# Attention loop written out, and probabilities times values as float32 products of 32 columns

## The chip, the core and the metric

The kernel runs on one core of a Trainium2 chip. The core has five engines that run side by side and wait for each other by semaphores: TensorE (PE in the profile; its weight loads are PEld), VectorE (DVE), ScalarE (ACT), GpSimd (POOL) and SyncE (SP), which here only issues transfers. Products are written to PSUM, the accumulation memory; everything else is read from SBUF. The metric is device time in microseconds, the median of three executions.

## The reference

A gated block in two parts, for 16 sequences of 256 tokens and width 512: cross attention with 16 heads of 32 columns and a causal mask, then a mixture of 8 experts, of which each token takes 6, and a shared expert. Only the attention is touched:

```python
q = x @ Wq.T;  k = context @ Wk.T;  v = context @ Wv.T
scores = jnp.einsum('bhqd,bhkd->bhqk', q, k) * SCALE
scores = jnp.where(causal[None, None, :, :], scores, -jnp.inf)
probs = jax.nn.softmax(scores, axis=-1)
y = jnp.einsum('bhqk,bhkd->bhqd', probs, v)
y = y.transpose(0, 2, 1, 3).reshape(b, t, c)
return y @ Wo.T + bo
```

with `x` replaced by its layer norm ahead of it and added to `tanh(g)` times the result behind it.

## The kernel before

`attention` works through the 16 sequences, called batches here. Each engine has its own program, in which `run(i)` stands for one turn and walks through 16 slots, `s` = 0 to 15, one for each head. In turn `i` the scores of batch `i` are made; between them, spread over the slots, stand the projections of batch `i + 1` (K in slots 0 to 3, Q in 4 to 7, V in 8 to 11) and the output projection of batch `i - 1` (slots 12 to 15). Turns run from -1 to 16. The order on each engine is thus written by hand; nothing is planned by costs. `iterations` (from line 226) writes turns -1 to 2 out, runs 3 to 12 in a loop of five passes of two turns over a register, and writes 13 to 16 out.

TensorE in slot `s` (`run`, from line 718): the scores of head `s`, two matmuls of 256 columns (L727), which contain three passes over stacked high and low parts; the products of probabilities and values of head `s - 4` (L744 to L746); three 128x128 transposes of the probabilities of head `s - 2` (L753); then the slot's part of a projection (L626 in `three_pass`, L616 for transposes). Full products are built from rounded parts: a value is split into a high and a low part, and hi x hi, hi x lo and lo x hi are summed.

Between the transposes and the products stand two engines. ScalarE copies the transposed probabilities to `pt_hi` in float16 (L452), VectorE subtracts it from PSUM for `pt_lo` (L591). Values are held in three bfloat16 parts in `v_parts`: ScalarE makes the first (L418), VectorE the remainder `v_rest` (L567), ScalarE the second from it (L422), GpSimd the third (L368). A head has three pairs of a query block and a key block below the diagonal, and each pair takes three 16-bit products: pt_hi with the first two parts (64 columns), pt_hi with the third (32), pt_lo with the first two (64). They fill two column groups in PSUM, which VectorE adds in `close_group` once for four heads (L531), before it multiplies by the inverse row sums (L535).

VectorE besides makes the mask, the maximum and the scaling of the scores (L559); ScalarE the exponentials (L457, L459). The experts' part (`experts`) holds the only float32 product of the kernel: `transpose_back` (L1174), in which four matmuls per block turn the logits back with the 16 rows of `fold`.

Of the kernel before, what the change touches and what calls it, by code (L numbers as in the profile page):

```python
# [21 lines left out]
F16 = mybir.dt.float16  # L22
# [6 lines left out]
P = 128  # L29
# [101 lines left out]
def attention(nc, ctx, memory, x, ctx_t, g_xattn, g_ffn, wq_t, wk_t, wv_t, wo_t, bo, x1, x1_stored, ident, gates, tanh_gates):  # L131
# [34 lines left out]
    v_parts = [sb(f"v_parts{i}", [P, T, 3, D], BF16) for i in range(2)]  # L166
    v_rest = sb("v_rest", [P, D])
    RING = 4
    probs = [sb(f"probs{i}", [P, 3 * P]) for i in range(RING)]
    pt_hi = [sb(f"pt_hi{i}", [P, 3 * P], F16) for i in range(2)]  # L170
    pt_lo = [sb(f"pt_lo{i}", [P, 3 * P], F16) for i in range(2)]
# [4 lines left out]
    y_sum = sb("y_sum", [P, T * JH, DH])  # L176
# [13 lines left out]
    y_ps = [psum(f"y{i}", [P, T, JH, 2, DH]) for i in range(2)]  # L190
# [8 lines left out]
    pool_chain, rstd_made, c_lo_made, v3_made = sem("pool_chain"), sem("rstd_made"), sem("c_lo_made"), sem("v3_made")  # L199
# [7 lines left out]
    v1_made, v2_made, yt_hi_made = sem("v1_made"), sem("v2_made"), sem("yt_hi_made")  # L207
    probs_made, pt_hi_made = sem("probs_made"), sem("pt_hi_made")
# [4 lines left out]
    v_rest_made, yt_lo_made, x1_made = sem("v_rest_made"), sem("yt_lo_made"), sem("x1_made")  # L213
    max_made, pt_lo_made, y_made = sem("max_made"), sem("pt_lo_made"), sem("y_made")
# [12 lines left out]
    FIRST, PAIRS = 3, 5  # L227

    def iterations(eng, run):

        for i in range(-1, FIRST):
            run(At(0, 2, i))
        with eng.Fori(0, PAIRS) as r:
            for u in range(2):
                run(At(r, 2, FIRST + u))
        for i in range(FIRST + 2 * PAIRS, B + 1):
            run(At(0, 2, i))
# [23 lines left out]
    V_SLOTS, V_EVAC, V_SPLIT = ((8, 9), (10, 11)), (10, 12), (11, 13)  # L263
# [17 lines left out]
    def build(start):  # L281
        with nc.Block() as block:
# [57 lines left out]
            def _(pool):  # L340
# [48 lines left out]
            def _(act):  # L389
# [19 lines left out]
                def run(i):  # L409
                    n, o, ln = i + 1, i + -1, i + 2  # L410
                    for s in range(H):
                        if has(i, 1):
                            if s in V_EVAC:
                                t, parts = V_EVAC.index(s), v_parts[n.parity()]
# [59 lines left out]
            def _(dve):  # L474
                NORM_STEPS = 2 * T + 2
                PER_GROUP = 2
# [45 lines left out]
                def close_group(b, g):  # L522

                    steps = PER_GROUP * (H // JH)
                    first, heads = PER_GROUP * g, slice(JH * g, JH * (g + 1))
                    dve.wait_ge(pv_done, b.times(H, JH * (g + 1)))
                    if g in (0, 2):
# [3 lines left out]
                    dve.tensor_reduce(y_sum[:], y_ps[g % 2][:].rearrange("p t h x d -> p (t h) d x"), AX.X,  # L531
                                      ALU.add).then_inc(group_chain, 1)
                    dve.wait_ge(group_chain, b.times(steps, first + PER_GROUP))
# [13 lines left out]
                def run(i):  # L547
                    n, o, ln = i + 1, i + -1, i + 2
                    for s in range(H):
# [12 lines left out]
                        if has(i, 1):  # L562
                            if s in V_EVAC:
                                t = V_EVAC.index(s)
                                dve.wait_ge(v1_made, n.times(T, t + 1))
                                wait(dve, v3_made, n.times(T, t))
                                dve.tensor_tensor(v_rest[:], bank[t][:], v_parts[n.parity()][:, t, 0, :],  # L567
                                                  ALU.subtract).then_inc(v_rest_made, 1)
# [40 lines left out]
            def _(pe):  # L609
# [40 lines left out]
                def units(i, s):  # L650
# [43 lines left out]
                    if has(i, -1):  # L694
                        if s in Y_SLOTS:
# [5 lines left out]
                            elif has(i, 1):  # L701
                                pe.wait_ge(v_rest_made, n.times(T, 1))
# [3 lines left out]
                        for t in range(T):  # L706
                            if s in O_SLOTS[t]:
# [4 lines left out]
                                elif half == 0 and has(i, 1):  # L712
                                    pe.wait_ge(v_rest_made, n.times(T, T))
# [556 lines left out]
```

## Time and profile before

| | |
|---|---|
| median of three runs | 2098.62 us (2096.86 to 2099.81) |
| profiled execution, span from first to last instruction | 2098.4 us |
| PE busy | 2029.4 us (97%), 12160 matmuls |
| DVE busy | 1148.4 us (55%) |
| ACT busy | 794.6 us (38%) |
| POOL busy | 192.7 us (9%) |

The page gives the span and no other time for the profiled execution. Busy shares are averages over two parts with different limits: attention ends near 698 us, the experts run from there to the end. Matmuls overlap in the records (one starts before the one ahead has left the array), so that the distance between two starts, and not the length of one, says what a matmul costs. A matmul whose weights are not loaded yet is recorded early and longer.

### The profile page before, as it was taken

The numbers are of one execution on the slowest core, as the hardware profiler recorded it, in microseconds if no ns is written. First come the engines' busy times: TensorE is split into PE (matmuls) and PEld (weight loads), VectorE is DVE, ScalarE is ACT, GpSimd is POOL, SyncE is SP. The second block draws the span as 40 slices with busy tenths as digits, with TensorE's granted clock in tenths as the row PEclk, the third lists the DMA queues.
The fourth block names the chain that finished last, engine by engine and source line by source line (L and its number), as shares of the span: only waits on it lengthen the run. The fifth ranks groups of instructions, "written<-read, shape, count | busy, mean of one in ns | idle before, by whom it ended". The sixth has DMA issues, their size and how long they took to land.

```text
span 2098.4 us, 34052 instructions
## 1 busy us (share of the span) xinstructions
PE 2029.4 (97%) x12160; PEld 1693.7 (81%) x12160; DVE 1148.4 (55%) x2766; ACT 794.6 (38%) x1974; POOL 192.7 (9%) x395
## 2 busy tenths in 40 slices
PE   6999898898998899999999999999999999999999
PEld 6899897898997678888888888777888888888887
DVE  5888787787888653334333433465334333433333
ACT  4777676676777441112121111153112111111111
POOL 3221221122220300000000000010000000000000
PEclk9999999999999899999999999999999999999999
DMA  7555554454544300000000100031001000000002
GB/s 206 132 132 143 122 132 115 119 143 118 134 119 126 130 21 21 28 23 31 20 20 20 30 20 28 19 125 51 23 28 31 21 20 20 30 20 20 20 1 80
DMA packets 117521, 138.56 MB, mean 66 GB/s; under 512 B 9728, under 2 KB 91648, under 8 KB 117376
## 3 DMA queue, kind: packets, MB, share of 16 engines
q1 hardware_dynamic: 117376, 136.63, 24.1%
q8 instruction: 90, 1.47, 0.3%
q14 instruction: 55, 0.45, 0.1%
HBM read 69.49 MB, written 16.78 MB: 41 GB/s over the span
## 4 chain that ended last, share of the span: by engine, by line
PE 61%; DMA 1%; DVE 1%; ACT 1%; POOL 1%; issue 1%; SPq 0%; POOLq 0%; DVEq 0%; ACTq 0%
PE gate_up L1190 40%; PE down L1209 20%; DMA acc<-x_between 1%; DMA out<-acc 1%; ACT xn L928 1%; DVE norm_stats L899 1%; POOL norm_newton L97 0%; PE gate_up L1167 0%; DVE xt_lo L1058 0%; PE down L1154 0%; PE gate_up L1174 0%; POOL norm_rstd L97 0%; POOL norm_newton L95 0%; ACT L1025 0%; DVE h L1097 0%
## 5 line engine op out<-in xcount | busy, mean ns | idle before, releaser
L1190 PE MATMUL gate_up<-xt_hi,e_hi 128*128 128x512 f32 x1280 | 507.2, 396 | 0.0
L1190 PE MATMUL gate_up<-xt_lo,e_hi 128*128 128x512 f32 x1280 | 506.3, 396 | 0.0
L1190 PE MATMUL gate_up<-xt_hi,e_lo 128*128 128x512 f32 x1280 | 506.3, 396 | 0.0
L1097 DVE TENSOR_TENSOR h<-gate_up,silu 128x512 f32<-128x512 f32 x160 | 110.6, 691 | 558.0 <-PE gate_up L1190 545.7
L1025 ACT ACTIVATE silu<-gate_up 128x512 f32<-128x512 f32 x160 | 95.7, 598 | 565.2 <-PE gate_up L1190 565.1
L1111 DVE SCALAR_TENSOR_TENSOR acc<-down,scale,acc 128x512 f32<-128x512 f32 x320 | 238.2, 749 | 109.2 <-PE down L1209 107.1
L1190 PEld LDWEIGHTS gate_up<-xt_lo,e_hi 128*128 128x128 f32 x1280 | 240.5, 188 | 58.3
L1190 PEld LDWEIGHTS gate_up<-xt_hi,e_hi 128*128 128x128 f32 x1280 | 240.5, 188 | 58.0
L1190 PEld LDWEIGHTS gate_up<-xt_hi,e_lo 128*128 128x128 f32 x1280 | 240.5, 188 | 57.6
L1028 ACT CAST h_hi<-h 128x512 fp32r<-128x512 f32 x160 | 99.4, 621 | 456.1 <-DVE h L1097 456.1
L1209 PE MATMUL down<-e_hi,h_hi 128*128 128x512 f32 x640 | 253.3, 396 | 0.9 <-DVE acc L1111 0.9
L1209 PE MATMUL down<-e_hi,h_lo 128*128 128x512 f32 x640 | 253.0, 395 | 0.0
L1209 PE MATMUL down<-e_lo,h_hi 128*128 128x512 f32 x640 | 252.8, 395 | 0.0
L559 DVE CUSTOM_DVE_ANT_0 probs<-scores,mask 128x128 f32<-128x128 f32 (+1 forms) x512 | 161.5, 352 | 95.1 <-PE scores L727 92.5
L1099 DVE TENSOR_TENSOR h_lo<-h,h_hi 128x512 fp32r<-128x512 f32 x160 | 110.8, 693 | 113.4 <-ACT h_hi L1028 113.4
L452 ACT CAST pt_hi<-probs_t 128x384 f16<-128x384 f32 x256 | 121.3, 474 | 79.5 <-PE probs_t L753 78.2
L591 DVE TENSOR_TENSOR pt_lo<-probs_t,pt_hi 128x384 f16<-128x384 f32 x256 | 140.6, 549 | 11.1 <-ACT pt_hi L452 10.6
L1209 PEld LDWEIGHTS down<-e_hi,h_hi 128*128 128x128 f32 x640 | 119.9, 187 | 31.0 <-issue 1.3
L727 PE MATMUL scores<-k_stack,q_stack 96*128 96x256 f32 x512 | 112.5, 300 | 32.7 <-issue 23.9
L1209 PEld LDWEIGHTS down<-e_hi,h_lo 128*128 128x128 f32 x640 | 120.0, 187 | 29.3
L1209 PEld LDWEIGHTS down<-e_lo,h_hi 128*128 128x128 f32 x640 | 120.0, 188 | 29.1
L753 PE MATMUL probs_t<-ident,probs 128*128 128x128 f32 x768 | 136.1, 287 | 0.3
(129 smaller groups left out, 3319.7 us busy)
## 6 DMA issues: line engine op xcount, KB each, us to landing
k_stack<-k_hi SPq DMA_DIRECT2D x128, 128.0 KB, 2.6
q_stack<-q_hi SPq DMA_DIRECT2D x128, 128.0 KB, 2.6
w_raw<-in_w_gate SPq DMA_DIRECT2D x20, 512.0 KB, 3.9
w_raw<-in_w_up SPq DMA_DIRECT2D x20, 512.0 KB, 3.9
w_raw<-in_w_down SPq DMA_DIRECT2D x20, 512.0 KB, 3.7
c_in<-in_ctx_t SPq DMA_DIRECT2D x16, 512.0 KB, 3.7
x_in<-in_x SPq DMA_DIRECT2D x16, 512.0 KB, 3.8
k_stack<-k_lo SPq DMA_DIRECT2D x64, 128.0 KB, 2.6
```

Source lines behind the costliest of these rows:

```text
L452: act.copy(pt_hi[h % 2][:], pt_ps[h % 2][:, 0:3 * P]).then_inc(pt_hi_made, 1)
L559: ins = dve.tensor_tensor_reduce(dst, sc_ps[s % 2][:, t, keys], mask[:, P * (1 - t):], -SCALE, -NEG, ALU.add, ALU.min, neg_max[:, s, t:t + 1])
L591: dve.tensor_tensor(pt_lo[h % 2][:], pt_ps[h % 2][:, 0:3 * P], pt_hi[h % 2][:], ALU.subtract).then_inc(pt_lo_made, 1)
L727: ins = pe.matmul(sc_ps[s % 2][:, t, :], q_stack[par][pairs, s, tile(t)], k_stack[par][pairs, s, :], start=True, stop=True)
L753: ins = pe.transpose(pt_ps[h % 2][:, tile(k)], probs[h % RING][:, tile(k)], ident[:])
L1025: act.activation(silu[f][:], gu_ps[f][:, 0, :], ACT.Silu).then_inc(silu_made, 1)
L1028: act.copy(h_hi[n.parity()][:, f, :], h[f][:]).then_inc(h_hi_made, 1)
L1097: dve.tensor_tensor(h[f][:], gu_ps[f][:, 1, :], silu[f][:], ALU.mult).then_inc(h_made, 1)
L1099: dve.tensor_tensor(h_lo[n.parity()][:, f, :], h[f][:], h_hi[n.parity()][:, f, :].bitcast(F32), ALU.subtract).then_inc(h_lo_made, 1)
L1111: dve.scalar_tensor_tensor(out=acc[slot(k)][:, t, :], in0=dn_ps[t][:], scalar=share_of, in1=acc[slot(k)][:, t, :], op0=ALU.mult, op1=ALU.a ...
L1190: ins = pe.matmul(gu_ps[f][:, which, :], (hi, lo)[a][:, c, f * P:(f + 1) * P], (xt_hi, xt_lo)[b][:, blk, c, :], start=(i == 0), stop=(i == ...
L1209: ins = pe.matmul(dn_ps[t][:], (h_hi, h_lo)[a][hp][:, f, t * P:(t + 1) * P], (hi, lo)[b][:, f, :], start=(i == 0), stop=(i == len(PASSES) ...
```

## The change

Two things are changed, both in `attention`. `iterations` writes all 18 turns out for every engine, without a loop. And the products of probabilities and values become float32 products: one copy by VectorE of the transposed probabilities (`pt`, now in float32) takes the place of `pt_hi` and `pt_lo`, one copy by ScalarE of the values (`values`) that of three parts on three engines, three products of 32 columns that of nine 16-bit ones, and the sum over two column groups in `close_group` goes. Waits for the parts become waits for the copies.

```diff
-    v_parts = [sb(f"v_parts{i}", [P, T, 3, D], BF16) for i in range(2)]
-    v_rest = sb("v_rest", [P, D])
+    values = [sb(f"values{i}", [P, T, D]) for i in range(2)]
...
-    pt_hi = [sb(f"pt_hi{i}", [P, 3 * P], F16) for i in range(2)]
-    pt_lo = [sb(f"pt_lo{i}", [P, 3 * P], F16) for i in range(2)]
+    pt = [sb(f"pt{i}", [P, 3 * P]) for i in range(2)]
...
-    y_ps = [psum(f"y{i}", [P, T, JH, 2, DH]) for i in range(2)]
+    y_ps = [psum(f"y{i}", [P, T, JH, DH]) for i in range(2)]
...
-    FIRST, PAIRS = 3, 5
-
     def iterations(eng, run):
-        for i in range(-1, FIRST):
-            run(At(0, 2, i))
-        with eng.Fori(0, PAIRS) as r:
-            for u in range(2):
-                run(At(r, 2, FIRST + u))
-        for i in range(FIRST + 2 * PAIRS, B + 1):
+        for i in range(-1, B + 1):
             run(At(0, 2, i))
...
(GpSimd)
-                        if s in V_SPLIT and has(i, 1):
-                            t, parts = V_SPLIT.index(s), v_parts[n.parity()]
-                            pool.wait_ge(v2_made, n.times(T, t + 1))
-                            pool.tensor_tensor(parts[:, t, 2, :], v_rest[:], parts[:, t, 1, :], ALU.subtract).then_inc(v3_made, 1)
...
(ScalarE)
-                                act.copy(parts[:, t, 0, :], bank[t][:]).then_inc(v1_made, 1)
-                            if s in V_SPLIT:
-                                t, parts = V_SPLIT.index(s), v_parts[n.parity()]
-                                act.wait_ge(v_rest_made, n.times(T, t + 1))
-                                act.copy(parts[:, t, 1, :], v_rest[:]).then_inc(v2_made, 1)
+                                act.copy(values[n.parity()][:, t, :], bank[t][:]).then_inc(values_made, 1)
...
-                        if (bh := lagging(i, s, TR_LAG)):
-                            b, h = bh
-                            act.wait_ge(pt_done, b.times(H, h + 1))
-                            wait(act, pv_done, b.times(H, h - 1))
-                            act.copy(pt_hi[h % 2][:], pt_ps[h % 2][:, 0:3 * P]).then_inc(pt_hi_made, 1)
...
(VectorE)
-                    dve.tensor_reduce(y_sum[:], y_ps[g % 2][:].rearrange("p t h x d -> p (t h) d x"), AX.X,
-                                      ALU.add).then_inc(group_chain, 1)
...
-                                      y_sum[:].rearrange("p (t h) d -> p t h d", t=T),
+                                      y_ps[g % 2][:],
...
-                            dve.wait_ge(pt_hi_made, b.times(H, h + 1))
-                            dve.tensor_tensor(pt_lo[h % 2][:], pt_ps[h % 2][:, 0:3 * P], pt_hi[h % 2][:],
-                                              ALU.subtract).then_inc(pt_lo_made, 1)
+                            dve.wait_ge(pt_done, b.times(H, h + 1))
+                            wait(dve, pv_done, b.times(H, h - 1))
+                            dve.tensor_copy(pt[h % 2][:], pt_ps[h % 2][:, 0:3 * P]).then_inc(pt_made, 1)
...
(TensorE)
-                            pe.wait_ge(pt_lo_made, b.times(H, h + 1))
+                            pe.wait_ge(pt_made, b.times(H, h + 1))
                             col = slice(h * DH, (h + 1) * DH)
                             for t, blocks in ((0, ((0, 0),)), (1, ((1, 0), (2, 1)))):
                                 for k, (blk, key) in enumerate(blocks):
-                                    last = k == len(blocks) - 1
-
-                                    dst = y_ps[g % 2][:, t, hg]
-                                    pe.matmul(dst, pt_hi[h % 2][:, tile(blk)], v[:, key, 0:2, col], start=(k == 0), stop=False)
-                                    pe.matmul(dst[:, 1], pt_hi[h % 2][:, tile(blk)], v[:, key, 2, col], start=False, stop=False)
-                                    ins = pe.matmul(dst, pt_lo[h % 2][:, tile(blk)], v[:, key, 0:2, col], start=False, stop=last)
+                                    ins = pe.matmul(y_ps[g % 2][:, t, hg], pt[h % 2][:, tile(blk)], v[:, key, col],
+                                                    start=(k == 0), stop=(k == len(blocks) - 1))
                             ins.then_inc(pv_done, 1)
```

TensorE in one slot with a part of the Q projection, before. The names are output<-moving operand, stationary operand; L727 are the scores, L744 to L746 the products, L753 the transposes, and a call that the chip executes in several instructions is one row here.

```order
L727 MATMUL scores<-k_stack,q_stack 128x256 [waits max_made]
L727 MATMUL scores<-k_stack,q_stack 128x256
L744 MATMUL y<-v_parts,pt_hi 128x64 [waits pt_lo_made]
L745 MATMUL y<-v_parts,pt_hi 128x32
L746 MATMUL y<-v_parts,pt_lo 128x64
L744 MATMUL y<-v_parts,pt_hi 128x64
L745 MATMUL y<-v_parts,pt_hi 128x32
L746 MATMUL y<-v_parts,pt_lo 128x64
L744 MATMUL y<-v_parts,pt_hi 128x64
L745 MATMUL y<-v_parts,pt_hi 128x32
L746 MATMUL y<-v_parts,pt_lo 128x64
L753 MATMUL probs_t<-ident,probs 128x128 [waits pt_lo_made,probs_made]
```

The same place of a slot in the changed kernel, where L692 are the scores, L706 the products and L714 the transposes.

```order
L692 MATMUL scores<-k_stack,q_stack 128x256 [waits max_made,stacked0_1]
L692 MATMUL scores<-k_stack,q_stack 128x256
L706 MATMUL y<-values,pt 128x32 [waits pt_made]
L706 MATMUL y<-values,pt 128x32 x2
L714 MATMUL probs_t<-ident,probs 128x128 [waits pt_made,probs_made]
L714 MATMUL probs_t<-ident,probs 128x128 x2
L591 MATMUL bank<-c_hi,w_hi 128x256
```

Nine rows of products have become three, at the same place between scores and transposes.

TensorE at the end of the loop's body before, from the last output projection of a turn to the first scores of the next pass.

```order
L626 MATMUL bank<-w_hi,t_lo 128x512
L626 MATMUL bank<-w_lo,t_hi 128x512
L235 REGISTER_ALU
L235 COMPARE_AND_BRANCH
L727 MATMUL scores<-k_stack,q_stack 128x256 [waits max_made,stacked1_0]
L727 MATMUL scores<-k_stack,q_stack 128x256
```

The same place of the changed kernel, between two turns.

```order
L591 MATMUL bank<-w_hi,t_lo 128x512
L591 MATMUL bank<-w_lo,t_hi 128x512
L692 MATMUL scores<-k_stack,q_stack 128x256 [waits max_made,stacked1_0]
L692 MATMUL scores<-k_stack,q_stack 128x256
L706 MATMUL y<-values,pt 128x32 [waits pt_made,y_made]
```

The register step and the branch are gone, and the scores follow the projection directly.

## Rows read from the trace of the kernel before

**Rows 1.** Windows: start:end length, then busy time of each engine, PEclk, DMA share, GB/s.

```profile
193.62:534.06 340.44, 316.51 (x3073) 290.51 (x3072) 271.61 (x913) 234.85 (x746) 78.19 (x136) 0.96 0.51 126
534.06:610.41 76.35, 76.35 (x770) 70.51 (x768) 67.60 (x229) 58.54 (x188) 19.56 (x34) 1.00 0.55 133
...
650.00:690.00 40.00, 30.75 (x296) 24.36 (x294) 33.59 (x118) 26.74 (x90) 7.34 (x8) 0.92 0.37 120
```

**Rows 2.** TensorE's waits over the whole run: us in total, times, longest.

```profile
PE scores L727 <- issue: 23.9, 8, 4.0
...
PE y L744 <- DVE pt_lo L591: 3.7, 9, 1.2
PE scores L727 <- DMA q_stack<-q_hi: 3.4, 1, 3.4
```

**Rows 3.** Timeline of TensorE around one jump: start, length, instructions, [idle before <-releaser].

```profile
234.40 0.38 PE L727 MATMUL scores<-k_stack,q_stack 96*128 96x256 f32 x1 [2.47 <-issue]
...
237.98 0.58 PE L727 MATMUL scores<-k_stack,q_stack 96*128 96x256 f32 x1 [3.20 <-issue]
```

**Rows 4.** Timeline of TensorE's matmuls in one slot of batch 7.

```profile
340.43 0.28 PE L626 MATMUL bank<-t_lo,w_hi 128*128 128x256 f32 x1
340.54 0.40 PE L727 MATMUL scores<-k_stack,q_stack 96*128 96x256 f32 x2
340.78 0.20 PE L744 MATMUL y<-v_parts,pt_hi 128*128 128x64 bf16 x1
...
341.02 0.19 PE L746 MATMUL y<-v_parts,pt_lo 128*128 128x64 bf16 x1
341.05 0.52 PE L753 MATMUL probs_t<-ident,probs 128*128 128x128 f32 x3
341.33 0.36 PE L626 MATMUL bank<-t_hi,w_hi 128*128 128x256 f32 x1
```

**Rows 5.** Timeline of the weight loads in the same slot.

```profile
340.43 0.31 PEld L727 LDWEIGHTS scores<-k_stack,q_stack 96*128 96x128 f32 x2
...
341.02 0.31 PEld L753 LDWEIGHTS probs_t<-ident,probs 128*128 128x128 f32 x3
341.30 0.19 PEld L626 LDWEIGHTS bank<-t_hi,w_hi 128*128 128x128 f32 x1
```

**Rows 6.** Timeline of TensorE's matmuls around a group of float32 products.

```profile
764.48 0.39 PE L1209 MATMUL down<-e_hi,h_lo 128*128 128x512 f32 x1
764.71 0.40 PE L1209 MATMUL down<-e_lo,h_hi 128*128 128x512 f32 x1
765.04 1.05 PE L1174 MATMUL gate_up<-fold,logits_t 16*128 16x8 f32 x8
766.02 0.50 PE L1209 MATMUL down<-e_hi,h_hi 128*128 128x512 f32 x1
```

**Rows 7.** Its loads in the timeline; then all of the line: min/median/max ns.

```profile
765.04 0.96 PEld L1174 LDWEIGHTS gate_up<-fold,logits_t 16*128 16x128 f32 x8 [0.37 <-issue]
...
L1174 PEld LDWEIGHTS gate_up<-fold,logits_t x64: 181/187/187, 707.6 to 1446.8; 16*128 16x128 f32 x64
L1174 PE MATMUL gate_up<-fold,logits_t x64: 251/251/273, 707.6 to 1446.8; 16*128 16x8 f32 x64
```

**Rows 8.** Groups by line: count | busy us, mean ns | idle before, releaser.

```profile
L591 DVE TENSOR_TENSOR pt_lo<-probs_t,pt_hi 128x384 f16<-128x384 f32 x256 | 140.6, 549 | 11.1 <-ACT pt_hi L452 10.6
...
L452 ACT CAST pt_hi<-probs_t 128x384 f16<-128x384 f32 x256 | 121.3, 474 | 79.5 <-PE probs_t L753 78.2
...
L531 DVE TENSOR_REDUCE y_sum<-y 128x256 f32<-128x512 f32 x64 | 40.9, 639 | 0.0
...
L567 DVE TENSOR_TENSOR v_rest<-bank,v_parts 128x512 f32<-128x512 f32 x32 | 22.0, 687 | 3.0 <-ACT v_parts L418 3.0
```

**Rows 9.** Timeline of TensorE in the last stage of attention, two scores in a row.

```profile
652.49 0.47 PE L727 MATMUL scores<-k_stack,q_stack 96*128 96x256 f32 x2 [0.84 <-DVE neg_max L559]
...
653.72 0.48 PE L727 MATMUL scores<-k_stack,q_stack 96*128 96x256 f32 x2
```

More of the change, by code:

```diff
@@ L198, in attention @@
     ident_made, mask_made, bias_made = sem("ident_made"), sem("mask_made"), sem("bias_made")
-    pool_chain, rstd_made, c_lo_made, v3_made = sem("pool_chain"), sem("rstd_made"), sem("c_lo_made"), sem("v3_made")
+    pool_chain, rstd_made, c_lo_made = sem("pool_chain"), sem("rstd_made"), sem("c_lo_made")
     res_made = sem("res_made")
@@ L206, in attention @@
     xt_hi_made, q_hi_made, k_hi_made = sem("xt_hi_made"), sem("q_hi_made"), sem("k_hi_made")
-    v1_made, v2_made, yt_hi_made = sem("v1_made"), sem("v2_made"), sem("yt_hi_made")
-    probs_made, pt_hi_made = sem("probs_made"), sem("pt_hi_made")
+    values_made, yt_hi_made = sem("values_made"), sem("yt_hi_made")
+    probs_made = sem("probs_made")
     w_lo_made, guess_made, norm_chain = sem("w_lo_made"), sem("guess_made"), sem("norm_chain")
@@ L212, in attention @@
     xt_lo_made, q_lo_made, k_lo_made = sem("xt_lo_made"), sem("q_lo_made"), sem("k_lo_made")
-    v_rest_made, yt_lo_made, x1_made = sem("v_rest_made"), sem("yt_lo_made"), sem("x1_made")
-    max_made, pt_lo_made, y_made = sem("max_made"), sem("pt_lo_made"), sem("y_made")
+    yt_lo_made, x1_made = sem("yt_lo_made"), sem("x1_made")
+    max_made, pt_made, y_made = sem("max_made"), sem("pt_made"), sem("y_made")
     xt_done, q_done, k_done, v_done = sem("xt_done"), sem("q_done"), sem("k_done"), sem("v_done")
@@ L262, in attention @@
     Q_SLOTS, Q_EVAC = (4, 5, 6, 7), (6, 8)
-    V_SLOTS, V_EVAC, V_SPLIT = ((8, 9), (10, 11)), (10, 12), (11, 13)
+    V_SLOTS, V_EVAC = ((8, 9), (10, 11)), (10, 12)
     Y_SLOTS, Y_EVAC, Y_BANKS = (8, 10), (9, 11), (BANK_B, BANK_A)
@@ L413, in run @@
                             if s in V_EVAC:
-                                t, parts = V_EVAC.index(s), v_parts[n.parity()]
+                                t = V_EVAC.index(s)
                                 act.wait_ge(v_done, n.times(T, t + 1))
@@ L475, in _ @@
                 NORM_STEPS = 2 * T + 2
-                PER_GROUP = 2
                 def statistics(ln):
@@ L522, in close_group @@
                 def close_group(b, g):
-                    steps = PER_GROUP * (H // JH)
-                    first, heads = PER_GROUP * g, slice(JH * g, JH * (g + 1))
+                    heads = slice(JH * g, JH * (g + 1))
                     dve.wait_ge(pv_done, b.times(H, JH * (g + 1)))
@@ L530, in close_group @@
                     dve.reciprocal(row_inv[:], row_sum[:, heads, :]).then_inc(group_chain, 1)
-                    dve.tensor_reduce(y_sum[:], y_ps[g % 2][:].rearrange("p t h x d -> p (t h) d x"), AX.X,
-                                      ALU.add).then_inc(group_chain, 1)
-                    dve.wait_ge(group_chain, b.times(steps, first + PER_GROUP))
+                    dve.wait_ge(group_chain, b.times(H // JH, g + 1))
                     part, at = (b.parity(), g * P) if g < 2 else (Y_LATE, (g - 2) * P)
                     dve.tensor_tensor(y[:, part, :, at:at + P].rearrange("p t (h d) -> p t h d", d=DH),
-                                      y_sum[:].rearrange("p (t h) d -> p t h d", t=T),
+                                      y_ps[g % 2][:],
                                       row_inv[:].rearrange("p h t -> p t h").unsqueeze(3).to_broadcast([P, T, JH, DH]),
@@ L562, in run @@
                         if has(i, 1):
[L563 to L568, printed above, removed]
                             if s in X_EVAC:
@@ L701, in units @@
                             elif has(i, 1):
-                                pe.wait_ge(v_rest_made, n.times(T, 1))
+                                pe.wait_ge(values_made, n.times(T, 1))
                             else:
@@ L712, in units @@
                                 elif half == 0 and has(i, 1):
-                                    pe.wait_ge(v_rest_made, n.times(T, T))
+                                    pe.wait_ge(values_made, n.times(T, T))
                                 ins = three_pass(bank[t][:], rows(t_hi, t_lo, tile(t)), weight(WO), HALF_CHUNKS[half])
@@ L731, in run @@
                             b, h = bh
-                            g, hg, v = h // JH, h % JH, v_parts[b.parity()]
+                            g, hg, v = h // JH, h % JH, values[b.parity()]
                             if h == 0:
-                                pe.wait_ge(v3_made, b.times(T, T))
+                                pe.wait_ge(values_made, b.times(T, T))
                             if hg == 0:
                                 wait(pe, y_made, b.times(H // JH, g - 1))
-                            pe.wait_ge(pt_lo_made, b.times(H, h + 1))
+                            pe.wait_ge(pt_made, b.times(H, h + 1))
                             col = slice(h * DH, (h + 1) * DH)
@@ L750, in run @@
                             pe.wait_ge(probs_made, b.times(H, h + 1))
-                            wait(pe, pt_lo_made, b.times(H, h - 1))
+                            wait(pe, pt_made, b.times(H, h - 1))
                             for k in range(3):
```

1 line of the change is left out of this document (removed).

## The prediction

> **What bounds the kernel now.** I read the windows by stage first, then TensorE's waits, then the timeline of one slot, and last the only float32 product that the kernel already has.
>
> The attention part runs to about 698 us, the experts fill the rest and are not touched. In the windows [rows 1] the two batches from 534.06 to 610.41 us take 76.35 us, TensorE is busy for all of it and its granted clock is 1.00. VectorE, the next engine, has 67.60 us of work there. So in the steady state TensorE is the bound, and what is added to its queue is added to the time.
>
> The window before it, 193.62 to 534.06, begins at the same matmul of a batch and holds eight batches, in the register loop: 340.44 us, 85.1 per two batches, with TensorE busy for 316.5 of them and a mean clock of 0.96. TensorE's waits name "issue" (nothing that the profile shows) in front of the scores, 23.9 us in 8 waits [rows 2]; two of them stand around one jump back, 2.47 us before the scores at 234.40 and 3.20 us before those at 237.98 [rows 3]. After such a pause the clock is granted at half, 1.2 GHz, for a stretch, which the mean of 0.96 says. Five passes have four jumps, all in that window.
>
> The last 40 us of attention are another stage: TensorE has 30.75 us of work there, VectorE 33.59 [rows 1].
>
> **The probability-value products on TensorE (the large term).** Per head the slot reads, in order, two scores matmuls, nine 16-bit products, three transposes, then the projection's matmuls [rows 4]. The second scores matmul starts 0.12 after the first and ends its stream 0.12 later, at 340.78, where the first product starts. The ninth starts at 341.02, and the transposes' weight load starts at once [rows 5]. Nine products take 340.78 to 341.02, 0.24 us, 0.03 each.
>
> The change issues three float32 products per head. The kernel has one float32 product today, the transposition of the logits with `fold`: four such calls in the code stand as eight matmuls and eight weight loads in the trace, so each float32 product is executed as two pairs of load and matmul [rows 7]. The eight loads last 0.96 us together and one lasts 0.187, so they start (0.96 - 0.187)/7 = 0.110 apart [rows 7]; the matmuls, (1.05 - 0.251)/7 = 0.114 apart [rows 6, 7]. Between the two I take 0.112. That is a load of 128 columns of 4 bytes; the 128-row loads of the projections agree, since the matmul at 341.33 has a load without cover, which starts at 341.30, and lasts 0.36 instead of the 0.28 of the same kind at 340.43: 0.03 from the load's start to the matmul's record and 0.08 of waiting in it make 0.11 [rows 4, 5].
>
> Is the matmul of 32 columns hidden in this pace? The transposes stream 128 float32 columns, and from the first to what follows the third it is 0.28 us [rows 4]: two streams at least lie in it, so at most 0.14 for 128 columns and 0.035 for 32. A load runs under the matmul ahead of it: the scores' loads begin at 340.43, when the last projection matmul begins, and the scores matmul follows 0.11 later at no cost [rows 4, 5]. So the 0.03 lies under the next 0.11, and the first of the six loads lies under the second scores matmul. The first new matmul starts at 340.78 as now, the sixth 5 x 0.112 = 0.56 later at 341.34, and the transposes' load with it, against 341.02 now. That is **+0.318 us per head**.
>
> The Trainium skill, "TensorE: Matmul & The Clock Gate", section "Measured speedup vs the span model", says that a load overlaps matmuls in flight only where the row group differs. The trace disagrees: the two scores matmuls, each with a load of its own, take 0.24 from 340.54 to 340.78, and the two loads start under the matmuls ahead [rows 4, 5]; loads of 0.11 and streams of 0.12 in turn would need 0.46. By that rule each pair would cost 0.14, which is inside the second rival.
>
> TensorE is the bound in batches 1 to 14 of the scores' turn: 14 x 16 = 224 heads x 0.318 = **+71.2 us**.
>
> **The edges.** In the first attention batch TensorE waits 3.4 us for the q_stack DMA, ahead of the next batch's scores [rows 2]. Queries are projected in slots 4 to 7, so the heads' products in these four push that DMA by 4 x 0.318 = 1.3 us, and the later ones are absorbed by the wait: **+1.3**. In the last stage the slots are 1.23 us apart [rows 9], of which TensorE fills 0.24 + 0.24 + 0.28 = 0.76; 0.318 more still fits in. There the path runs through ScalarE's pt_hi (0.474) and VectorE's pt_lo (0.549) [rows 8], and the first of them goes. Four or five slots there have output-projection work and pay in full; the relief of the shorter path and of the sum over two columns at the end (0.639) comes off. Bounds: 20 heads x 0.318 = +6.4, and -3.7, all that TensorE waits for pt_lo now [rows 2]. I take **+1.0**.
>
> **The loop written out.** The eight batches with the four jumps take 340.44 - 4 x 76.35 = 35.0 us more than eight written-out ones would, stalls and slow clock together [rows 1]. The same code written out, 534.06 to 610.41 us, shows no idle time of TensorE at all, so nothing takes its place: **-35.0 us**. Bounds: 0 (the longer code stalls as often) and -35.0.
> The Trainium skill, "Advanced Engine Details and Errata", section "Control Flow Timing", puts a compare-and-branch at about 108 ns. By that figure four jumps would be an estimated 0.4 us and the sum 34.6 us higher; the trace has some 8.8 us per jump, so the stall is not the branch itself and the trace decides.
>
> **VectorE, ScalarE, GpSimd.** VectorE loses 64 sums of 0.639 and 32 remainders of v of 0.687 and exchanges 256 subtractions of 0.549 for copies of the same 384 columns [rows 8]. If a copy costs as much as the subtraction, 62.9 us go, if it costs what ScalarE's does (0.474), 82. ScalarE loses the 256 pt_hi copies (121.3 us) and 32 copies of v; GpSimd loses v's third part. None of them bounds a slot: all of it is worth **0**, since TensorE's queue, 76.35/32 = 2.39 us per slot [rows 1], covers it, now and more so after. The copy now waits for TensorE's transposes directly, and behind it on VectorE stand the group's closing and the next mask-and-maximum; the transposes end 0.32 later in a slot that is 0.32 longer, and the products need the copy two slots later. Bounds 0 and, if VectorE were late once per batch by one copy, +9.
>
> **Sum.** 71.2 + 1.3 + 1.0 - 35.0 = +38.5. The profiled execution's span is 2098.4 us, 0.2 under the median of the three runs (2098.62); the page has no other time for it. 2098.4 + 38.5 + 0.2 = 2137.1, and I say **2137 us**, slower by 1.8%.
>
> **Rivals.**
> *Float32 products drain the array at both ends.* Around the eight fold pairs there are gaps: the matmul ahead starts at 764.71 and streams for 0.23 (its distance to the one before), yet the first fold load starts only at 765.04, 0.10 late; and from there eight loads of 0.112 end at 765.94, where the next matmul starts at 766.02, about 0.09 late as well [rows 6, 7]. If float32 is the cause, each head pays 2 x 0.092 and the uncovered first load of 0.110: 0.318 + 0.294 = 0.612, x 224 = 137.1, and with the edges (+3) and the loop 2098.6 + 140 - 35 = **2204 us**. Against it: fold has 16 rows and all its neighbours 128, so the height may be the cause; transposes, float32 too, stand between 16-bit and projection matmuls without a gap.
> The Trainium skill, "TensorEngine Tiling (Array Packing)", section "Key Properties", states that a change of tiling mode drains TensorE. That fits a 16-row product between 128-row ones, and would leave the new products, of 128 rows, without a gap; the trace's scores of 96 rows show none either.
> *No cover.* The first load carries the wait for the copy, or the 32-column stream does not lie under the next load: 0.110, or 5 x 0.03 = 0.15, more per head. 224 x 0.13 = 29 more: **2166 us**. For it: the first 16-bit load starts only when the scores' stream is over. Against it: the transposes' load carries a wait and starts at once [rows 5].
> *The stalls stay.* The longer code is fetched with the same pauses: 2137.1 + 35.0 = **2172 us**. Against it the windows of written-out batches.
> *Faster.* The float32 loads run at the pace of the transposes' loads, which start faster: three last 0.31 together and the last 0.14, so two starts lie in 0.17, and one of them holds a stream of 128 columns, 0.11; that leaves 0.06 [rows 5]. Six pairs then end 5 x 0.06 = 0.30 after the scores, +0.06 per head, 13 us in all against 35: **2078 us**. It turns at 35.0/224 = 0.156 per head, a pace of (0.24 + 0.156)/5 = 0.08 per pair. For it: only 16-row float32 loads of this kind are in the trace. Against it: 0.110 there and the same 0.11 on the 128-row loads of the projections.
>
> **Chances.** The forecast 0.52 (its own range 2128 to 2150, from a pace of 0.107 to 0.118 and the edges), the drain 0.16, no cover 0.14, the stalls staying 0.06, faster 0.08, the rest 0.04 spread on both sides. The range runs from 2122 to 2208: it takes in the forecast, no cover, the stalls and the drain, and leaves out faster and the rest. A measurement of this kernel can tell 0.2% (4 us) from no change. Slower 0.89, same 0.02, faster 0.09.
>
> **What would show it.** In the profile after, 1536 float32 matmuls of 32 columns for the products, at 0.112 from one to the next; transposes whose load starts 0.56 us after the first product; two batches in 76.35 + 32 x 0.318 = 86.5 us with the clock at 1.00 throughout; no issue wait before scores. TensorE still full there. A gap of 0.09 ahead of the first product load would show the drain; a first product that starts 0.11 after its load and after the scores' end, no cover; a pace under 0.08 would make the forecast wrong in sign.

## The result, and the profile after

| | before | after |
|---|---|---|
| median of the timed runs | 2098.31 us (2096.86 to 2099.81, 4 runs) | 2135.46 us (2134.19 to 2136.63, 4 runs) |
| span of the profiled execution | 2098.4 us | 2132.1 us |
| PE busy | 2029.4 us (97%) | 2095.9 us (98%) |
| matmuls | 12160 | 11392 |

After to before is 1.0172, interval 1.0158 to 1.0187: slower by 37 us, where 38.5 were forecast. Each ratio further down is against executions of the kernel before taken beside that run, with medians of 2099.0 to 2100.4 us. The head of the page after:

```profile
span 2132.1 us, 30972 instructions
...
PE 2095.9 (98%) x11392; PEld 1777.8 (83%) x11392; DVE 1090.3 (51%) x2670; ACT 687.0 (32%) x1686; POOL 152.7 (7%) x363
```

The windows of the same stages as in [rows 1] (start:end length, busy time of each engine, granted clock, DMA share, GB/s): eight batches, then the next two, then the last stage.

```profile
209.27:556.31 347.04, 347.04 (x2689) 329.70 (x2688) 243.17 (x864) 180.95 (x600) 58.43 (x120) 1.00 0.50 122
556.31:643.07 86.76, 86.76 (x673) 82.42 (x672) 60.78 (x216) 45.23 (x150) 14.60 (x30) 1.00 0.47 116
686.45:737.84 51.39, 42.08 (x288) 38.08 (x286) 37.78 (x132) 25.94 (x80) 10.84 (x20) 0.87 0.38 126
```

TensorE is busy in every one of the 347.04 us at a clock of 1.00, and eight batches take exactly four times the 86.76 us of two. VectorE, ScalarE and GpSimd have less to do than before, and with TensorE full that cannot shorten this stage.

One slot, TensorE's matmuls and then its loads, as in [rows 4, 5]:

```profile
361.29 0.40 PE L692 MATMUL scores<-k_stack,q_stack 96*128 96x256 f32 x2
361.53 0.75 PE L706 MATMUL y<-values,pt 128*128 128x32 f32 x6
362.12 0.53 PE L714 MATMUL probs_t<-ident,probs 128*128 128x128 f32 x3
362.40 0.48 PE L591 MATMUL bank<-w_hi,c_hi 128*128 128x512 f32 x1
```

```profile
361.41 0.76 PEld L706 LDWEIGHTS y<-values,pt 128*128 128x128 f32 x6
361.64 0.53 PEld L706 LDWEIGHTS y<-values,pt 128*128 128x128 f32 x4
362.01 0.40 PEld L714 LDWEIGHTS probs_t<-ident,probs 128*128 128x128 f32 x3
...
L706 PEld LDWEIGHTS y<-values,pt 128*128 128x128 f32 x1536 | 195.2, 192 | 0.3 <-DVE pt L557 0.3
```

Three products are six pairs. The first load starts at 361.41, under the second scores matmul (it is covered, as I call it from here on), and the first product at 361.53, when that stream ends: nothing is lost at the seam. The last four loads are (0.53 - 0.192)/3 = 0.113 apart. From the first product to the transposes it is 0.59 us, against 0.27 in [rows 4]: +0.32 per head. The copy costs VectorE 551 ns, as much as the subtraction it replaced (549 in [rows 8]), and the products waited for it 0.3 us in the whole run.

Where the 33.7 us between the two spans come from:

| stage | before | after | difference |
|---|---|---|---|
| batches 1 to 14, at the written-out pace | 38.18 each | 43.38 each | 14 x 5.20 = +72.9 |
| jumps of the loop | 35.0 | 0 | -35.0 |
| start of attention | | | -0.35 |
| last stage | 54.78 | 51.39 | -3.4 |
| experts and rest | | | -0.4 |

### The profile page after: what moved, and what is told of

Its sections match the earlier page's. It is cut to its first block, busy times and chain, and to the rows that moved or that the text cites. A ratio compares the mean times of both kernels' runs of the same rounds, so it can differ in the third digit from the quotient of the medians.

```text
span 2132.1 us, 30972 instructions
## 1 busy us (share of the span) xinstructions
PE 2095.9 (98%) x11392; PEld 1777.8 (83%) x11392; DVE 1090.3 (51%) x2670; ACT 687.0 (32%) x1686; POOL 152.7 (7%) x363
## 4 chain that ended last, share of the span: by engine, by line
PE 60%; DMA 1%; DVE 1%; ACT 1%; POOL 1%; issue 1%; SPq 0%; POOLq 0%; DVEq 0%; ACTq 0%
PE gate_up L1151 40%; PE down L1170 20%; DMA acc<-x_between 1%; ACT xn L889 1%; DVE norm_stats L860 1%; DMA out<-acc 0%; PE gate_up L1128 0%; POOL norm_newton L97 0%; DVE xt_lo L1019 0%; PE down L1115 0%; PE gate_up L1135 0%; POOL norm_rstd L97 0%; POOL norm_newton L95 0%; ACT L986 0%; DVE h L1058 0%
## 5 line engine op out<-in xcount | busy, mean ns | idle before, releaser
L706 PEld LDWEIGHTS y<-values,pt 128*128 128x128 f32 x1536 | 195.2, 192 | 0.3 <-DVE pt L557 0.3
L706 PE MATMUL y<-values,pt 128*128 128x32 f32 x1536 | 193.5, 262 | 0.1
L432 ACT ACTIVATE probs<-probs,neg_max 128x128 f32<-128x128 f32 x256 | 103.1, 403 | 223.8 <-DVE neg_max L530 223.5
L557 DVE COPY pt<-probs_t 128x384 f32<-128x384 f32 x256 | 141.1, 551 | 11.9 <-PE probs_t L714 1.0
```

What stands on the lines that cost most here:

```text
L432: act.activation(p[:, 0:P], p[:, 0:P], ACT.Exp, bias=neg_max[:, s, 0:1], scale=-1.0, accum_out=row_sum[:, s, 0:1])
L557: dve.tensor_copy(pt[h % 2][:], pt_ps[h % 2][:, 0:3 * P]).then_inc(pt_made, 1)
L706: ins = pe.matmul(y_ps[g % 2][:, t, hg], pt[h % 2][:, tile(blk)], v[:, key, col], start=(k == 0), stop=(k == len(blocks) - 1))
```

## Experiments: the two parts apart

**Only the loop written out** (e1_unroll_only; before, 16-bit products kept):

```
-            for i in range(-1, FIRST): run(At(0, 2, i))
-            with eng.Fori(0, PAIRS) as r:
-                for u in range(2): run(At(r, 2, FIRST + u))
-            for i in range(FIRST + 2 * PAIRS, B + 1): run(At(0, 2, i))
+            for i in range(-1, B + 1): run(At(0, 2, i))
```

> The kernel before with the attention loop written out on all engines, the 16-bit products kept. My theory (the two parts of the change are separate terms): 2098.3 - 35.0 = 2063 us, batches 38.15 us apart throughout, no issue wait before scores. Rival (the longer code of nine products per head is fetched with pauses, and the changed kernel escaped them only through its shorter code): pauses of some microseconds stay, 2070 to 2098 us.

Measured: 2063.57 us (2062.63 to 2065.52), ratio 0.9832 (0.9814 to 0.9849). The eight batches that took 340.44 us now take 305.18, at full clock and with no issue wait:

```profile
191.69:496.87 305.18, 305.15 (x3074) 282.27 (x3072) 270.66 (x913) 233.84 (x746) 78.03 (x136) 1.00 0.57 139
```

So on 16-bit products the written-out loop is worth the 35 us that the windows gave.

**Only the float32 products** (e2_float_in_loop; after, with the register loop put back by the reverse of that edit):

> The changed kernel with the register loop put back, the float32 products kept. My theory (separate terms): 2135.5 + 35.0 = 2170 us, window of eight batches in the loop 8 x 43.38 + 35 = 382 us. Rival (the jump's cost depends on the work around it, so that slower slots hide a part of it): 2150 to 2160 us. If the parts are separate, this run minus the kernel before is the price of the products alone, 72 us.

Measured: 2135.28 us (2134.53 to 2135.73), ratio 1.0171 (1.0152 to 1.0189), against 2135.46 for after. This broke my theory that the two terms stand apart. Five passes with four jumps, and not one stall in the window of the same eight batches:

```profile
209.69:556.73 347.04, 347.04 (x2689) 329.71 (x2688) 242.57 (x864) 180.89 (x600) 58.12 (x120) 1.00 0.49 121
```

| | register loop | written out |
|---|---|---|
| 16-bit products | 2098.3 | 2063.6 |
| float32 products | 2135.3 | 2135.5 |

The loop edit brings 35 us in the upper row and nothing in the lower. The float32 products have fewer instructions (6 pairs per head instead of 9). Something in the jump must depend on that, and the transfers hint at what. From its second pass on, over seven batches (234.40 to 534.06 us), before had (queue, kind: packets, MB, share of the DMA engines)

```profile
q1 hardware_dynamic: 33566, 36.69, 50.0%
q8 instruction: 32, 0.52, 0.7%
q14 instruction: 18, 0.15, 0.2%
```

and after with its loop back has, over the same seven batches (253.07 to 556.73 us),

```profile
q1 hardware_dynamic: 33600, 36.71, 49.0%
```

that is, no instruction transfers at all. The q8 transfers of before are 16 KB each, about nine per pass. New theory: where a pass is short enough, its instructions stay on the chip and a jump back is free. Rival: the stall comes with the 16-bit code for another reason, such as VectorE's or ScalarE's own jumps.

## Experiments: what the jump costs, and when

**Only TensorE written out** (e3_tensor_unrolled) and **all but TensorE written out** (e4_others_unrolled), both on before:

```
+            if eng is nc.tensor:          # e4: eng is not nc.tensor
+                for i in range(-1, B + 1): run(At(0, 2, i))
+                return
```

> The kernel before, written out on TensorE alone; the four other engines keep their loop. Theory (the pause is TensorE's own, at its jump, and the others' pauses are hidden by TensorE's queue): 2063 to 2067 us, nearly all of the 35 us. Rival (the pause is one of VectorE's or ScalarE's, on which the scores wait): 2090 us or more, with TensorE waiting for neg_max or the copies at the same places.

> The kernel before, written out on the four other engines; TensorE alone keeps its loop. Theory (TensorE's own jump is the pause): 2095 to 2099 us, the same as before. Rival (the others' jumps are the cause): 2063 to 2070 us. If both this and the run with TensorE alone written out stay slow, each kind of jump is enough by itself.

Measured: e3 2077.11 us (2076.78 to 2079.4), ratio 0.9897 (0.9879 to 0.9915); e4 2100.79 us, ratio 1.0005 (0.9995 to 1.0014). TensorE's own jump makes the stall: with it alone, the issue waits of [rows 2] stand as they were, in e4:

```profile
PE scores L731 <- issue: 24.5, 8, 4.0
```

Behind such a stall the clock falls: from 236 to 243 us in before, behind the first jump, the granted clock is 0.52, so mostly 1.2 GHz, and TensorE had done 3.33 us of work in the 9 us from 231 to 240.

But e3 recovers only 22 of the 35 us and ends 10 us above the range I gave. Without its stall TensorE meets the jumps of the others: it waits for t_lo, which VectorE makes, once behind each jump.

```profile
PE bank L630 <- DVE t_lo L523: 9.7, 4, 2.5
```

So the jumps of the other engines cost about 13 us as well once they are exposed (2077.1 against 2063.6). In before they lay under TensorE's. They are no fixed price either: in e2 the same four engines jump as often, TensorE's list of waits is empty, and no instruction transfer is left on q14 either, where e3 still has 19 in seven batches, with an issue wait of VectorE once per jump (4.6 us in 4). Which property of the four bodies makes the difference was not separated.

**A shorter body** (f1_body1446, f2_body1574; before with its loop, and fewer products in a pass). A pass of before issues 1638 instructions on TensorE: 1536 matmuls and loads, some 100 waits and register operations. After with its loop back (e2) has 1447, as many as f1 within one; f2 has 1574.

```
-   pe.matmul(dst[:, 1], pt_hi[h % 2][:, tile(blk)], v[:, key, 2, col], start=False, stop=False)
```
(f1: the line is gone; f2: it stands behind `if blk > 0:`)

> The kernel before, loop kept, without the product of pt_hi with the third part of the values (L745), which leaves that part out of the result. Per pass of the loop TensorE's program has 192 instructions less, 1446 instead of 1638, against 1447 in the changed kernel with its loop put back, which had no pause at the jump. Theory (TensorE's pause depends on how many instructions the loop's body has, since a body that is small enough is not fetched anew): no issue wait before scores and no instruction transfer for TensorE after the first pass; VectorE's and ScalarE's jumps cost what they cost when TensorE alone was written out, so 2077 minus 3 x 0.028 x 230 = 19, 2058 us. Rival (the pause belongs to the 16-bit products and their short instructions): pauses stay, 2099 - 19 = 2080 us.

> As the run before, but the product is left out for two of the three block pairs' worth less: it stays for blocks 1 and 2 and goes for block 0 only, so the body has 1574 instructions; the result lacks the third part of the values for block 0. This places the limit between 1447 (no pause) and 1638 (pause). If 1574 is still over the limit: pauses and 16 KB transfers in each pass, 2099 - 0.028 x 230 = 2092 us. If it is under: 2077 - 6 = 2071 us.

Measured: f1 2072.01 us (2070.28 to 2075.45), ratio 0.9869 (0.9853 to 0.9886); f2 2078.56 us (2077.26 to 2081.24), ratio 0.9896 (0.988 to 0.9913). The register loop and the 16-bit products are there in both, yet the issue waits are gone and so are the q8 transfers. Of f2, from the second pass on (229.78 to 513.13 us):

```profile
q1 hardware_dynamic: 33615, 36.73, 53.2%
q14 instruction: 19, 0.16, 0.2%
```

That is the mechanism, and for this loop the limit lies between 1574 and 1638 TensorE instructions per pass. What is left is TensorE waiting for VectorE behind the jumps, as in e3; in f2:

```profile
PE bank L626 <- DVE t_lo L519: 9.9, 4, 2.6
```

The sizes were missed: I had 2058 and 2071. The traces show where. A batch without a jump, in f1 and in f2:

```profile
266.65:304.19 37.54, 37.22 (x338) 33.97 (x337) 33.57 (x115) 28.85 (x94) 9.78 (x17) 1.00 0.57 140
272.28:310.25 37.97, 37.97 (x369) 34.81 (x368) 33.74 (x115) 29.18 (x95) 9.77 (x17) 1.00 0.57 138
```

Against 38.15 in e1 that is 0.6 and 0.2 us less, 8 and 3 us in fourteen batches, where I had taken off 19 and 6. In f1 TensorE is idle for 0.3 us of the batch, so VectorE has begun to set the pace; the rest of the missing gain is open. And the eight batches with the four jumps take 315.28 and 321.31 us, 15 and 18 more than eight such batches, where the same comparison gives 13 in e3.

The Trainium skill, "Advanced Engine Details and Errata", section "ISA Cache", gives TensorE 128 KB in lines of 16 KB, 256 instructions each. The 16 KB transfers here agree. From that size one would estimate that 2048 instructions stay, and the runs show fetching already at 1638, so the page's size does not predict the limit; why it is lower is open.

**A longer body on float32** (f3_four_turns; after, in two passes of four batches, some 2890 instructions and one jump):

```
+            with eng.Fori(0, 2) as r:
+                for u in range(4): run(At(r, 4, FIRST + u))
```

> The changed kernel with a loop of two passes of four turns: a body of some 2890 instructions on TensorE and one jump. Theory (size of the body): one pause of about 8.8 us with issue waits before the scores of turn 7, 2135.4 + 8.8 = 2144 us. Rival (float32 products, whose slots are longer and whose instructions come more slowly, hide the fetch at a jump): 2135 us, no pause.

Measured: 2143.88 us (2141.0 to 2145.51), ratio 1.0208 (1.0191 to 1.0226), 8 us more than after. The two batches around the jump take 92.44 us instead of 86.76, at a lower clock, and the issue waits are back (the first line is the window, the others the waits):

```profile
295.33:387.77 92.44, 88.73 (x674) 83.94 (x672) 60.74 (x216) 45.21 (x150) 14.53 (x30) 0.98 0.47 116
PE y L713 <- issue: 2.2, 1, 2.2
PE scores L699 <- issue: 1.5, 1, 1.5
```

So it is the length of the body and not the kind of product. The window is 5.7 us longer and the profiled execution 7.2 (2139.3 against 2132.1). TensorE's waits for xn and for its own sequencer, both in the experts' part, are 2.4 us longer than in after, which can make the difference; a link of theirs to the jump is not shown.

## Experiments: what sets the price of a product

**Four times the columns** (e5_cols128; each product streams 128 columns instead of 32):

```
-   pe.matmul(y_ps[g % 2][:, t, hg], pt[..][:, tile(blk)], v[:, key, col], ...)
+   pe.matmul(y_ps[g % 2][:, t].rearrange("p h d -> p (h d)"), pt[..][:, tile(blk)], v[:, key, g*P:(g+1)*P], ...)
```

> The changed kernel with float32 products of 128 columns instead of 32 (all four heads of a group at once, each head overwriting the others' columns, so the attention result is wrong for three heads in four). Theory (the stream of a product lies under the next load): 128 float32 columns stream for 0.107 by the transposes' distance, just under the load's 0.110, so only the last one shows, 0.045 per head, about 10 us: 2145 us. Rival (load and stream in turn, the forecast's price being right by chance): 6 x 0.08 per head, 110 us more, 2245 us.

Measured: 2145.69 us (2145.59 to 2145.78), ratio 1.0214 (1.0193 to 1.0234). A batch takes 44.08 us instead of 43.38, 0.044 more per head, as the theory has it for the last product of a head alone. The six loads of a head still last 0.76 us together, as in after. So a stream of up to 128 columns lies under the next load.

**Three pairs per head instead of six** (f4_reduced; `values` and `pt` typed as reduced float32):

```
-    pt = [sb(f"pt{i}", [P, 3 * P]) for i in range(2)]        # and values
+    pt = [sb(f"pt{i}", [P, 3 * P], F32R) for i in range(2)]
```

> The changed kernel with probabilities and values rounded to the reduced float32 format (float32r), so that a product is one pair of load and matmul: three loads per head instead of six; the products are less exact. Theory (the products cost their loads, 0.112 each, the first one covered): 3 x 0.112 x 230 = 77 less, 2135.4 - 77 = 2058 us, 5 us under the 16-bit products written out, of which 4 from the shorter path at the end. Rival (a float32 product costs its four passes of 32 columns and not its loads): the single pass would take 3 x 0.013, 2000 us or less.

Measured: 2062.44 us (2062.08 to 2064.2), ratio 0.9821 (0.9804 to 0.9837).

```profile
350.07 0.41 PE L706 MATMUL y<-values,pt 128*128 128x32 f32 x3
350.32 0.55 PE L714 MATMUL probs_t<-ident,probs 128*128 128x128 f32 x3
```

Three pairs take 0.25 us where after takes 0.59 and before 0.27. With e5 beside it, the price is the number of float32 loads; the number of columns hardly counts.

**Half the load** (e6_half_load; the stationary operand has 64 columns; the rows of PSUM that are no longer written are set to zero once at the start):

```
-   pe.matmul(y_ps[g % 2][:, t, hg], pt[..][:, tile(blk)], v[:, key, col], ...)
+   pe.matmul(y_ps[g % 2][0:64, t, hg], pt[..][:, blk * P:blk * P + 64], v[:, key, col], ...)
```

> The changed kernel with products whose stationary operand has 64 columns instead of 128 (the other half of each query block is left out). Theory (a float32 load costs 0.11 for 128 columns and in proportion): pace 0.056 instead of 0.112, 5 x 0.056 = 0.28 per head less, 64 us: 2071 us. Rival (a pair of instructions has a price of its own, whatever the columns): 2135 us.

Measured: 2132.07 us (2131.56 to 2132.59), ratio 1.0149 (1.0129 to 1.0169), 61 us over what I expected. The loads do go at half price, (0.42 - 0.138)/5 = 0.056 apart:

```profile
342.24 0.42 PEld L708 LDWEIGHTS y<-values,pt 128*64 128x64 f32 x6
342.71 0.31 PEld L716 LDWEIGHTS probs_t<-ident,probs 128*128 128x128 f32 x3
```

```profile
341.83 0.48 PE L694 MATMUL scores<-k_stack,q_stack 96*128 96x256 f32 x2
342.25 0.54 PE L708 MATMUL y<-values,pt 128*64 128x32 f32 x6
```

But the second scores matmul starts at 342.03 and has streamed by 342.15, and the first load starts at 342.24, 0.09 later, no longer under the stream. The sixth load is over near 342.58, and the transposes' load starts at 342.71. The two gaps and the uncovered load eat the 0.28 that the halves save.

**Half the rows** (e7_rows64; operands of 64 rows):

```
-   pe.matmul(y_ps[g % 2][:, t, hg], pt[..][:, tile(blk)], v[:, key, col], ...)
+   pe.matmul(y_ps[g % 2][:, t, hg], pt[..][0:64, tile(blk)], v[0:64, key, col], ...)
```

> The changed kernel with products over 64 rows instead of 128 (half of each key block is left out), all else alike. The gaps of 0.09 at both ends of the fold products were not there at the new products of 128 rows. Theory (a change of the height of the operand, as 16 rows between 128, empties the array): 0.09 at both ends and the first load uncovered, 0.29 per head, 70 us: 2205 us. Rival (the gaps at fold have another cause): 2135 us, first product as close to the scores as now.

Measured: 2227.24 us (2225.88 to 2228.6), ratio 1.0602 (1.0581 to 1.0623). The same gaps now stand on full-price loads:

```profile
360.53 0.40 PE L692 MATMUL scores<-k_stack,q_stack 96*128 96x256 f32 x2
360.86 0.85 PE L706 MATMUL y<-values,pt 64*128 64x32 f32 x6
361.64 0.55 PE L714 MATMUL probs_t<-ident,probs 128*128 128x128 f32 x3
```

The second scores matmul has streamed by 360.77, the first load comes at 360.86. A batch takes 48.20 us, 4.82 more than after, 67.5 in fourteen. Another 22 us are in the last stage, which takes 54.32 us where after takes 32.55 for the same work, at a granted clock of 0.63 instead of 0.98, so largely at 1.2 GHz, although TensorE is busy for 53.22 of the 54.32 us:

```profile
757.68:812.00 54.32, 53.22 (x247) 46.21 (x245) 27.14 (x100) 17.85 (x68) 2.49 (x2) 0.63 0.26 88
```

Both executions of e7 show the lower clock: 0.985 and 0.986 over the whole run, against 0.994 in after. What brought it down was not separated.

The two together answer the drain rival. A change of the operand's height (64 rows next to 128 here, 16 in [rows 6]) or of the stationary width (64 next to 128 columns) costs some 0.09 us ahead and 0.1 behind, plus the cover of the first load; float32 by itself costs neither. The Trainium skill, "TensorEngine Tiling (Array Packing)", section "Key Properties", has the drain at a change of tiling mode, without a price. These runs agree with it by their gaps of 0.09 us, and the 96-row scores next to 128 rows show none.

## Experiment: a version faster than both

Float32 is the dear way to save instructions. The other is to drop the values' third 16-bit part (g1_two_parts; before with the loop written out, two float16 parts for the values, and neither the third part nor the product with it; waits for the third part become waits for the second):

```
-    v_parts = [sb(f"v_parts{i}", [P, T, 3, D], BF16) for i in range(2)]
+    v_parts = [sb(f"v_parts{i}", [P, T, 2, D], F16) for i in range(2)]
-                            pool.tensor_tensor(parts[:, t, 2, :], v_rest[:], parts[:, t, 1, :], ALU.subtract).then_inc(v3_made, 1)
-                                    pe.matmul(dst[:, 1], pt_hi[h % 2][:, tile(blk)], v[:, key, 2, col], start=False, stop=False)
```

> A version meant to beat both kernels: the 16-bit products with the loop written out, and the values in two float16 parts instead of three bfloat16 ones, so that a block pair takes two products (64 columns each) instead of three, and GpSimd's third part goes. Theory (TensorE is the bound in the steady state and the third product costs 0.028): 3 x 0.028 x 230 = 19 less than the written-out kernel's 2063.6, but the run without L745 gained only 1.0 us per batch, as VectorE then comes late now and then: 2049 us. Rival (VectorE is the bound as soon as TensorE has less): 2060 us or more.

Measured: 2049.67 us (2048.33 to 2052.0), ratio 0.9760 (0.9744 to 0.9777).

```profile
223.71:521.87 298.16, 296.63 (x2689) 271.66 (x2688) 263.79 (x915) 233.98 (x744) 58.17 (x120) 1.00 0.58 142
```

Eight batches take 298.16 us, 37.27 each. That is 2.4% under before and 4% under after. VectorE is now busy for 88% of the stage, and TensorE has begun to wait for it (2.2 us for q_lo in the attention part), so I expect little more from shortening TensorE's work alone; no run tests that.

## Why the prediction was right, and where it was not

- **The products, +71.2: right, measured +72.9.** Three products are executed as six pairs of load and matmul, 0.112 apart, with the stream below the load (e5) and the first load below the scores. The price per head in the slot is the forecast 0.318; the eight batches give 5.20/16 = 0.325. The difference of 0.007 per head is below what the slot's rows, read to 0.01, can place. One marker was off: the transposes' load starts 0.48 after the first product, not 0.56, since the second product is recorded right behind the first and the transposes' matmul only 0.11 after their load.
- **The loop, -35.0: the amount was right, its cause only in part.** I took it as a price of the jump that writing the loop out removes. It is a price of a body too long to stay on the chip, and the shorter float32 body had already removed it (e2). On its own the loop edit is worth 35 us on before (e1) and nothing here; the products alone cost 37, their 72 less the 35. The sum came out right because the stall was taken off once, whichever part removes it. The window that I took for written-out code, 534.06 to 610.41, holds the last turn of the loop as well as the first one behind it; it has no jump back, and e1's 305.18 us for eight batches confirm its pace.
- **VectorE, ScalarE, GpSimd, 0: right.** The products wait 0.3 us for the copy in all.
- **The first batch, +1.3: wrong, about 0.** The scores of batch 1 start 0.35 us earlier than before (76.01 instead of 76.36). The twelve heads whose products stand ahead of them add 12 x 0.32 = 3.8 us of work. The q_stack wait did not shrink, 3.7 us instead of the 3.4 of [rows 2]. But TensorE's listed waits in the first 80 us went from 19.7 to 18.4 us, and its granted clock between 40 us and that start from 0.92 to 0.97; an estimate from these is 1.3 and some 1.8 us, most of the work added.
- **The last stage, +1.0: wrong in sign, -3.4.** In [rows 9] two scores are 1.23 apart; now 1.19, and TensorE no longer waits there for pt, 3.7 us in [rows 2]:

```profile
688.76 0.48 PE L692 MATMUL scores<-k_stack,q_stack 96*128 96x256 f32 x2
689.95 0.49 PE L692 MATMUL scores<-k_stack,q_stack 96*128 96x256 f32 x2
```

  The lower bound of -3.7, all of that wait, was the better value.
- **From the span to the run, +0.2: wrong, 3.4 (2135.46 less 2132.1).** The timed runs lie some 2 us over their own spans (a run of after of 2134.3 has a span of 2132.1), so before's profiled execution was some 2 us above its median, and after's was 1.2 below. Between the two spans the change is 33.7 us, 4.8 less than the forecast sum; between the medians it is 37.15, since the two profiled executions lay on different sides of theirs. That the total comes within 1.4 us of 38.5 is luck in that part: the edges were 6 us too high, the products 1.7 too low, and the step from span to median made up 3.4.

Of the rivals, the drain is refuted for 128 rows and 128 stationary columns and shown for 64 of either (e6, e7). No cover is refuted by the load at 361.41. The stalls do not stay, in either form of the loop. The faster pace of 0.06 belongs to loads of 64 columns (e6), and its gaps undo it. The sentence of the Trainium skill that a load overlaps matmuls in flight only where the row group differs stands in the page "TensorE: Matmul & The Clock Gate" in the section "The mechanism", not in the one that the prediction names; the load at 361.41, 0.12 us before the end of the stream ahead of it, contradicts it for this kernel.

## What to carry to other kernels

Count load and matmul pairs before columns: here a full float32 product is two loads of 0.112 us whatever it streams up to 128 columns, so three of them cost more than nine 16-bit ones, and halving the operand buys nothing where it breaks the cover of its neighbours. Two edits that remove the same stall must not be added up: run each alone, and look in the trace at whether instruction transfers go on after the first pass before a loop is written out. Where TensorE is full for a whole stage, do not count on work taken off the other engines.

## What the runs showed of the hardware

- TensorE's own jump back leaves no issue wait at 1446, 1447 and 1574 TensorE instructions per pass, and costs 8.8 us (35.0/4, slow clock included) at 1638. Up to 1574 no q8 instruction transfer follows the first pass; at 1638 there are about nine of 16 KB in every pass.
- The jumps of the four other engines together cost some 3 us per pass in e3 (13/4) and 4 in f1 and f2. They cost nothing where TensorE's stall covers them (before), and nothing in e2, where no instruction transfers follow the first pass.
- A change of height or of stationary width between neighbouring products costs about 0.09 us before and 0.1 behind, and the cover of the first load.
- With 64-row products the granted clock fell to 0.63 in the last stage, where it is 0.98 with 128 rows. Both executions of e7 have the lower mean clock; its cause was not separated.
